# A gate on four column groups, a first norm in blocks of four tiles, and loads behind the identity

## What is computed

```python
x = x + 0.5 * _L0_ffn_ref(_layernorm(x, axis=-1), ...)
x = x + _L0_attn_ref(_layernorm(x, axis=-1), ...)
x = x + 0.5 * _L0_ffn_ref(_layernorm(x, axis=-1), ...)

def _L0_ffn_ref(x, gate_w, gate_b, w1, b1, w2, b2, w3, b3):
    logits = jnp.einsum('bsd,de->bse', x, gate_w) + gate_b
    probs = jax.nn.softmax(logits, axis=1)
    vals, idx = jax.lax.top_k(probs, K)
    ...
```

## Time and profile before

| | us |
|---|---|
| median of 3 runs | 2303.44 (2300.15 to 2309.62) |
| the profiled execution, its own time | 2308.49 |
| its span | 2306.7 |
| PE busy in the span | 2189.5 (95%) |
| DVE busy | 1855.1 (80%) |
| ACT busy | 1608.6 (70%) |
| POOL busy | 534.6 (23%) |

### The profile page before, as it was taken

The page is one execution under the profiler, slowest core; times in us unless marked ns, Lnnn a source line. Parts: engine busy times, 40 slices in busy tenths (PEclk is TensorE's granted clock), DMA queues, the critical chain, the costliest instruction groups (busy, mean ns, idle before and its releaser), DMA issues.

```text
span 2306.7 us, 97898 instructions
## 1 busy us (share of the span) xinstructions
PE 2189.5 (95%) x42417; PEld 1911.3 (83%) x42417; DVE 1855.1 (80%) x3872; ACT 1608.6 (70%) x3516; POOL 534.6 (23%) x1311
## 2 busy tenths in 40 slices
PE   5699988999999999999999999999999998879997
PEld 4588876469899999999999999998999996768885
DVE  4655556599999999999999999999999993465555
ACT  2244444478888888888888888888888886234442
POOL 1233311331221312212212212222122111023330
PEclk7599999999999999999999999999999999769998
DMA  6311112420100100101101001011010003031112
GB/s 201 104 48 46 46 19 72 135 68 8 31 22 13 31 11 25 30 5 32 24 11 31 15 20 31 6 29 27 8 31 22 13 4 112 1 113 48 48 46 81
DMA packets 95464, 96.23 MB, mean 42 GB/s; under 512 B 41269, under 2 KB 84025, under 8 KB 95033
## 3 DMA queue, kind: packets, MB, share of 16 engines
q0 software_dynamic: 42048, 44.80, 7.8%
q1 hardware_dynamic: 52016, 44.10, 6.1%
q10 hardware_dynamic: 968, 1.06, 0.1%
HBM read 64.14 MB, written 25.43 MB: 39 GB/s over the span
## 4 chain that ended last, share of the span: by engine, by line
PE 93%; DVE 3%; ACT 2%; issue 2%; POOL 1%; DMA 0%; ACTq 0%; POOLq 0%; DVEq 0%
PE bank L1016 42%; PE bank L1008 18%; PE bank L917 18%; PE bank L971 2%; PE bank L877 2%; PE bank L1054 2%; PE bank L928 1%; PE bank L984 1%; PE bank L1119 1%; PE bank L855 1%; PE bank L897 1%; PE bank L935 1%; ACT feat L684 1%; PE bank L1062 1%; DVE x_res L1411 0%
## 5 line engine op out<-in xcount | busy, mean ns | idle before, releaser
L1016 PE MATMUL bank<-work 96*32 96x512 bf16 (+4 forms) x17920 | 1415.3, 363 | 4.9 <-DVE work L1450 3.6
L793 ACT ACTIVATE feat<-bank 128x512 f32<-128x512 f32 (+3 forms) x2304 | 1251.4, 565 | 155.3 <-PE bank L1016 78.2
L1450 DVE TENSOR_REDUCE work<-bank 128x1 f32<-128x512 f32 (+3 forms) x2176 | 1299.8, 640 | 64.7 <-PE bank L1016 52.9
L1008 PE MATMUL bank<-feat,phase 128*17 128x128 f32 x16896 | 1138.9, 272 | 1.1 <-issue 1.1
L1008 PEld LDWEIGHTS bank<-feat,phase 128*17 128x17 f32 x16896 | 829.3, 98 | 67.2 <-issue 2.3
L1016 PEld LDWEIGHTS bank<-work 96*32 96x32 bf16 (+1 forms) x17920 | 809.8, 96 | 72.3 <-DVE work L1450 13.2
L917 PE MATMUL bank<-work 128*128 128x256 f32 x1872 | 434.7, 382 | 3.4 <-issue 2.7
L917 PEld LDWEIGHTS bank<-work 128*128 128x128 f32 x1872 | 340.5, 191 | 53.6 <-issue 12.1
L1348 DVE COPY work<-phase 128x514 f32 x234 | 100.6, 430 | 189.6 <-ACT work L742 57.4
L555 POOL TENSOR_SCALAR_AFFINE_SELECT feat<-feat 128x128 f32<-128x128 f32 x512 | 147.2, 295 | 446.0 <-ACT feat L793 437.2
L497 POOL DMA_INDIRECT work<-token_table,row_no x156 | 149.0, 955 | 327.8 <-DVE work L1362 240.9
(11 more groups left out here) (169 smaller groups left out, 1484.2 us busy)
## 6 DMA issues: line engine op xcount, KB each, us to landing
phase<-in_w SPq DMA_DIRECT2D x12, 1024.0 KB, 11.9
work<-qk_parts POOLq DMA_DIRECT2D x60, 192.0 KB, 4.2
token_table<-rows SPq DMA_DIRECT2D x8, 1056.0 KB, 8.8
qk_parts<-phase SPq DMA_DIRECT2D x20, 384.0 KB, 2.6
work<-qk_parts POOLq DMA_DIRECT2D x60, 128.0 KB, 4.5
qk_parts<-work SPq DMA_DIRECT2D x12, 384.0 KB, 3.0
x_res<-in_x SPq DMA_DIRECT2D x4, 1024.0 KB, 13.3
work<-work SPq DMA_DIRECT2D x256, 1.0 KB
```

The source lines that it names most:

```text
L793: eng.activation(p_ring[:, n % P_RING, lo:QB], s_bank("probs", n)[:, lo:QB], ACT.Exp, scale=HD ** -0.5).then_inc(sig.s_done, 1)
L1008: mm = eng.matmul(bank[ACC_BANK][GRID * g:GRID * g + VW, 0:P], v_aug[:, t, h, :], p_ring[:, n % P_RING, g * P:(g + 1) * P], start=(t == 0) ...
L1016: mm = eng.matmul(out[GRID * g:GRID * (g + 1), width], left[:, GRID * g:GRID * (g + 1)], right, start=start, stop=stop)
L1450: eng.tensor_reduce(maxima[:, h % 2, j, i, k + 1:k + 2], scores[:, 0:hi - lo], AX_X, ALU.max).then_inc(sig.a_done, 1)
```

## The change

1. The first norm goes by 8 groups of 4 tiles, and x comes in 8 DMAs of 4 tiles.
2. SP waits after the first of these loads until POOL has built the identity (`ident_at`); seven loads of x, the expert weights, the biases and now `w_qkv_sb` and `w_out_sb`, which were ACT's, come behind that wait. ACT issues the two small gate loads only; the gate's weights wait for a memset of DVE, since they now have 32 columns, of which 24 are zero. The rows of zeros are stored behind the first norm.
3. The transposes wait for the identity alone, no longer for all constants.
4. The gate is turned round. The gate's weights (128x32) stand still, and 128 tokens move; four tiles go to four column groups of PE and four 32-partition strips of bank 2. ACT copies the 128x128 result to `gate_t`, and one matmul per block of four tiles, with `gate_t` as weights against 32 columns of the identity, puts the logits back with tokens on partitions, in bank 7.
5. In both norms with a gate, the gate of a block stands behind other work: in the first norm behind the next block's transposes; in the third behind the output projection of the group after.
6. `H_BANKS` loses bank 7: two banks take turns for the heads' transposes.

```diff
-LN_GRP = (GRP, 4, GRP)
+LN_GRP = (4, 4, GRP)
+GATE_TILES, GATE_W = 4, 32
+GATES = NT // GATE_TILES
-H_BANKS = (3, 6, 7)
+H_BANKS = (3, 6)
...
             triangle(ident[:, :], 0.0, ALU.not_equal, 1.0)
+            ident_at[0] = n_const[0]
...
-            for g in range(GROUPS):
-                eng.dma_start(x_res[:, g * GRP:(g + 1) * GRP, :],
-                              x_rows[:, g * GRP:(g + 1) * GRP, :]).then_inc(sig.x_loaded[g], 16)
+            for g in range(NT // LN_GRP[0]):
+                a, b = g * LN_GRP[0], (g + 1) * LN_GRP[0]
+                if g == 1:
+
+                    need.wait_ge(sig.const, ident_at[0])
+                eng.dma_start(x_res[:, a:b, :], x_rows[:, a:b, :]).then_inc(sig.x_loaded[g], 16)
             load_experts(0)
+            eng.dma_start(w_qkv_sb[:, :, :], w_qkv_t.rearrange("(k p) o -> p k o", p=P)).then_inc(sig.attw, 16)
+            eng.dma_start(w_out_sb[:, :, :], w_out_t.rearrange("(k p) o -> p k o", p=P)).then_inc(sig.attw, 16)
...
         def _(eng):
             need = Waits(eng)
-            eng.dma_start(gate_w_sb[:, :, :], gate_w.rearrange("(k p) e -> p k e", p=P)).then_inc(sig.small, 16)
             eng.dma_start(gate_b_sb[:, :], gate_b.partition_broadcast(P)).then_inc(sig.small, 16)
-            eng.dma_start(w_qkv_sb[:, :, :], w_qkv_t.rearrange("(k p) o -> p k o", p=P)).then_inc(sig.attw, 16)
-            eng.dma_start(w_out_sb[:, :, :], w_out_t.rearrange("(k p) o -> p k o", p=P)).then_inc(sig.attw, 16)
+            need.wait_ge(sig.gate_pad, 1)
+            eng.dma_start(gate_w_sb[:, :, 0:E], gate_w.rearrange("(k p) e -> p k e", p=P)).then_inc(sig.small, 16)
...
+            def copy_gate(f, m):
+
+                need.wait_ge(sig.gate_t[f], m + 1 if f == 0 else m // 2 * 2 + 2)
+                need.wait_ge(sig.gate[f], m - 1)
+                eng.activation(gate_t[:, m % 2, :], bank[2][:, m % 2 * P:(m % 2 + 1) * P],
+                               ACT.Copy).then_inc(sig.gate_copy[f], 1)
+
+            def first_norm():
+                sqrt_of(0, 0)
+                for m in range(GATES):
+                    if m + 1 < GATES:
+                        sqrt_of(0, m + 1)
+                    copy_feat(0, m)
+                    if m:
+                        copy_gate(0, m - 1)
+                copy_gate(0, GATES - 1)
...
             def transpose_rows(n, g):
-                need.wait_ge(sig.const, n_const[0])
+                need.wait_ge(sig.const, ident_at[0])
...
+            def gate(f, m):
+
+                need.wait_ge(sig.small, 32)
+                need.wait_ge(sig.feat[2 * f], KD * (m + 1))
+                need.wait_ge(sig.gate_copy[f], m if f == 0 else m // 2 * 2)
+                if f == 1:
+                    need.wait_ge(sig.s_done, S_ALL)
+                for k in range(KD):
+                    for g in range(GATE_TILES):
+                        i = GATE_TILES * m + g
+                        mm = eng.matmul(bank[2][GATE_W * g:GATE_W * (g + 1), m % 2 * P:(m % 2 + 1) * P],
+                                        gate_w_sb[:, k, :], feat[:, k, i * P:(i + 1) * P], start=(k == 0),
+                                        stop=(k == KD - 1))
+                mm.then_inc(sig.gate_t[f], 1)
+
+            def gate_rows(f, m):
+
+                need.wait_ge(sig.gate_copy[f], m + 1)
+                width = GATE_TILES * E
+                eng.matmul(bank[7][:, m * width:(m + 1) * width], gate_t[:, m % 2, :],
+                           ident[:, :].rearrange("p (c w) -> p c w", c=GATE_TILES)[:, :, 0:E], start=True,
+                           stop=True).then_inc(sig.gate[f], 1)
+
+            def first_norm():
+                for m in range(GATES):
+                    transpose_rows(0, m)
+                    if m:
+                        gate(0, m - 1)
+                    if m > 1:
+                        gate_rows(0, m - 2)
+                gate_rows(0, GATES - 2)
+                gate(0, GATES - 1)
+                gate_rows(0, GATES - 1)
+
             def layer_norm(n, add, consume):
                 add(0)
                 groups = NT // LN_GRP[n]
                 for g in range(groups):
                     if g + 1 < groups:
                         add(g + 1)
+                    if n == 2 and g:
+                        gate(1, 2 * g - 2)
+                        gate(1, 2 * g - 1)
                     transpose_rows(n, g)
+                    if n == 2 and g:
+                        gate_rows(1, 2 * g - 2)
+                        gate_rows(1, 2 * g - 1)
                     consume(g)
+                if n == 2:
+                    gate(1, GATES - 2)
+                    gate(1, GATES - 1)
+                    gate_rows(1, GATES - 2)
+                    gate_rows(1, GATES - 1)
...
-            layer_norm(0, nothing, lambda g: gate(0, g))
+            first_norm()
...
+            def first_norm():
+                statistics(0, 0)
+                for g in range(GATES):
+                    if g + 1 < GATES:
+                        statistics(0, g + 1)
+                    normalise(0, g)
...
-            layer_norm(0, nothing, nothing)
+            eng.memset(gate_w_sb[:, :, :], 0.0).then_inc(sig.gate_pad, 1)
+            first_norm()
```

More of the change, by code:

```diff
@@ L209, in __init__ @@
         self.const = one("constants")
-        self.x_loaded = many("x_loaded", GROUPS)
-        self.small = one("small_loads")
+        self.x_loaded = many("x_loaded", NT // LN_GRP[0])
+        self.gate_pad, self.small = one("gate_padded"), one("small_loads")
         self.attw = one("attention_weights")
@@ L328, in macaron_block @@
         v_rest = sb("v_rest", [P, D])
+        gate_t = v_rest[:, :].rearrange("p (b s) -> p b s", b=2)
         wat = [0]
@@ L658, in _, with store_zero_rows @@
             need = Waits(eng)
-            eng.dma_start(gate_w_sb[:, :, :], gate_w.rearrange("(k p) e -> p k e", p=P)).then_inc(sig.small, 16)
             eng.dma_start(gate_b_sb[:, :], gate_b.partition_broadcast(P)).then_inc(sig.small, 16)
-            eng.dma_start(w_qkv_sb[:, :, :], w_qkv_t.rearrange("(k p) o -> p k o", p=P)).then_inc(sig.attw, 16)
-            eng.dma_start(w_out_sb[:, :, :], w_out_t.rearrange("(k p) o -> p k o", p=P)).then_inc(sig.attw, 16)
-            need.wait_ge(sig.const, zeros_at[0])
-            for f in range(2):
-                eng.dma_start(table[f][0:1, :].rearrange("o (a b) -> (o a) b", a=2),
-                              zeros_bf[:, :].bitcast(F32)[0:2, 0:ROW // 2]).then_inc(sig.zero, 16)
+            need.wait_ge(sig.gate_pad, 1)
+            eng.dma_start(gate_w_sb[:, :, 0:E], gate_w.rearrange("(k p) e -> p k e", p=P)).then_inc(sig.small, 16)
+            def store_zero_rows():
+                need.wait_ge(sig.const, zeros_at[0])
+                for f in range(2):
+                    eng.dma_start(table[f][0:1, :].rearrange("o (a b) -> (o a) b", a=2),
+                                  zeros_bf[:, :].bitcast(F32)[0:2, 0:ROW // 2]).then_inc(sig.zero, 16)
             def sqrt_of(n, g):
@@ L697, in layer_norm @@
                     consume(g)
+                if n == 2:
+                    copy_gate(1, GATES - 2)
+                    copy_gate(1, GATES - 1)
             def nothing(g):
@@ L710, in route @@
                                bc(chosen[:, :, :], 2, [P, NT, V_ROWS // E, E]), ACT.Copy).then_inc(sig.chosen_wide[f], 1)
-                need.wait_ge(sig.gate[f], NT * KD)
+                need.wait_ge(sig.gate[f], GATES)
                 for m in range(NT // 4):
@@ L863, in layer_norm @@
                         add(g + 1)
+                    if n == 2 and g:
+                        gate(1, 2 * g - 2)
+                        gate(1, 2 * g - 1)
                     transpose_rows(n, g)
+                    if n == 2 and g:
+                        gate_rows(1, 2 * g - 2)
+                        gate_rows(1, 2 * g - 1)
                     consume(g)
+                if n == 2:
+                    gate(1, GATES - 2)
+                    gate(1, GATES - 1)
+                    gate_rows(1, GATES - 2)
+                    gate_rows(1, GATES - 1)
             def nothing(g):
                 return
-            def gate(f, g):
-                need.wait_ge(sig.small, 32)
-                need.wait_ge(sig.feat[2 * f], 2 * KD * (g + 1))
-                if f == 1:
-                    need.wait_ge(sig.s_done, S_ALL)
-                for i in range(g * GRP, (g + 1) * GRP):
-                    for k in range(KD):
-                        eng.matmul(bank[2][:, i * E:(i + 1) * E], feat[:, k, i * P:(i + 1) * P], gate_w_sb[:, k, :],
-                                   start=(k == 0), stop=(k == KD - 1)).then_inc(sig.gate[f], 1)
             def route(f):
@@ L882, in route @@
                 need.wait_ge(sig.routed[f], ROUTED["chosen_bf"])
+                need.wait_ge(sig.const, n_const[0])
                 if f == 1:
@@ L1127, in _ @@
             attention()
-            layer_norm(2, attended, lambda g: gate(1, g))
```

(5 more changed lines are left out.)

10 lines of the change are left out of this document (7 added, 3 removed).

## The result

| | before | after |
|---|---|---|
| median of four runs each, us | 2302.44 (2300.15 to 2309.62) | 2265.09 (2264.18 to 2265.92) |
| ratio, 95% interval | | 0.9825 (0.981 to 0.9841) |
| profiled execution, its span | 2308.49, 2306.7 | 2265.92, 2264.2 |
| logits of the first norm (DVE's first routing step) | 64.27 | 45.82 |
| last attention matmul | 1933.98 | 1909.94 |

The change gains 37.4 us by the medians: 18.45 in the first norm and 18.75 in the third. (The profiled pair is 42.6 apart. 5.8 of it lie in attention, 1596.5 us before and 1590.7 after, where the program is the same; they belong to those two executions, see gate_alone_again.)

A forecast was written before the change was run, and what follows sets the result against it. The prediction took PE as the bound in both norms with a gate, and DVE as the first norm's new bound. Gains of 21 us (first norm) and 17 (third), 38 in all, took 2303.4 to 2265.4 us; range 2257 to 2279.

The forecast's parts named there:

- The bound moves to DVE: First norm: with the new gate DVE sets the pace at 3.55 us a block, PE about level at 3.6.
- Rival (b): Gate's column groups do not overlap, or shape changes cost a microsecond: only 10 us gained, 2293 us; chance 0.07.
- (c): Gate's column groups quite serial at low clock, a block costing PE over 6 us: slower, 2317 us; chance 0.02.
- The change of shape: PE at the new gate: switching to column groups and back costs 0.19 us for both changes together.
- The first norm: Logits of the first norm at 43.2 us instead of 64.3: 21 us gained.
- I take half, 6.1: POOL's 12.26 us wait before the identity's select halves to 6.1 without the long loads; identity ready at 7.6 us.
- the "1.0" for POOL's wide copies: First norm: 1.0 us added for DVE's work being slowed beside POOL's wide copies.
- Rival (a): First norm: POOL's wait is its own and stays at 12.26 us; 15 us gained instead of 21, 2271.5; chance 0.27.
- The third norm: Third norm's logits at about 1995.3 us instead of 2012.3: 17 us gained, between 10 and 20.
- The granted clock at 1.00 up to the last projection, and low in the tail: Third norm: PE's clock holds full until the last projection, then is low, costing another 1.5 us.
- its debits: Third norm: 0.6 us once for two head banks, and up to 2 us for ACT's later square root at low clock.
- that walk along PE's list: Third norm: PE's work summed from 1957.05 at full clock, ending the last projection at 1981.0 us instead of 1992.1.

The follow-up runs named there:

- gate_alone_again: Repeat of gate_alone, the same kernel on another chip: 2264.92 us, 0.985 for gate_alone and 0.9835 here, against the kernel before.
- loads_alone: Changed kernel with the old gate's matmuls, in the third norm straight behind their transposes, and three banks for the heads: 2299.27 us, 0.9964 of the kernel before.
- identity_first: Changed kernel with SP's wait for the identity put ahead of the first load of x too: 2261.57 us (one run).
- after_again: The changed kernel, unaltered, run again in another group: 2264.91 us, 0.9835 of the kernel before.
- all_at_once: Changed kernel without SP's wait for the identity, so all loads are issued at once: 2260.38 us, 0.9812 of the kernel before.
- gate_in_place: Changed kernel with the third norm's gate and turning back right behind the transposes they read: 2270.36 us, 0.984 of the kernel before.
- gate_alone: Changed kernel with the kernel before's four loads of x, no SP wait, attention weights in ACT's queue, transposes waiting for all constants: 2273.68 us, 0.985 of before.
- wide_copies_late: Changed kernel with POOL's two wide copies held until DVE has written all rows of the first norm: 2268.42 us, 0.9847 of the kernel before.
- copies_in_gaps: Changed kernel with each of POOL's wide copies waiting for a group of DVE's rows, to meet the next statistics: 2262.56 us, 0.9823 of before.

## Why the prediction was right

The median came out at 2265.09, forecast 2265.4. The sum hides two misses that cancel, and each of its steps had an answer of its own.

**The bound moves to DVE: right.** DVE has no holes from block 1 on, PE waits for it in every block, and loads_alone shows the other side: with the old gate PE stays the bound. Rival (b), column groups that do not overlap, and (c), a block of over 6 us, are out: 16 records take 0.57 us at the higher level and 1.08 at the lower, against 0.55 and 1.1 taken from attention's row. The turning back of two blocks took 0.37 us from start to start in the third norm (1950.12 to 1950.49), 0.19 a block, forecast 0.22.

**The change of shape: right.** The last block's 8 transposes and the change behind them took 1.01 us (41.95 to 42.96) where 8 transposes of the heads take 0.87: 0.14 at most for the change to column groups; the one back lies in the gate's 0.57, taken as 0.55. Both were put at 0.19. The Trainium skill (TensorEngine Tiling (Array Packing), Key Properties) says the array drains at a change; this trace does not contradict it, but shows no price above 0.14 us for the change to column groups.

**The first norm: 18.45 gained, not 21.** The step that failed is the identity: "I take half, 6.1" of the 12.26 us. identity_first shows 6.86 for the part that stays without long loads, and one block of x beside it makes it 8.37 here, and 7.8 to 8.0 in five other kernels with the same loads, after_again among them. That makes the landing of block 1 13.89 instead of 12.0, 2.3 too late by the identity and 0.4 less by the load behind it (3.93 instead of 4.4). The second term that was mis-sized is the "1.0" for POOL's wide copies: it cost 2.4, since it met four rows, not the small operation that the row showed. DVE's blocks of 3.43 instead of 3.55 gave 0.6 back. 2.3 - 0.4 + 1.4 - 0.6 - 0.1 (tail 3.93 instead of 4.0) = 2.6: logits at 45.82, forecast 43.2. Rival (a), the wait unchanged at 12.26, was wrong for these loads, but would have done no harm where DVE had x: all_at_once had 10.98.

**What the prediction did not ask** is whether the wait for the identity is worth its price. It priced parts 2 and 3 as part of one sum, with DVE's start at the landing of block 1, and had both numbers at hand: DVE needs x from the start, the identity only for PE, a block later. gate_alone_again and all_at_once give the answer: the transposes' wait for the identity alone, with the smaller loads, is worth 5.0 us at the logits (44.82 to 39.86), and SP's wait gives 6.0 back (45.82). The 5.0 hold the attention weights' move from ACT's queue to the end of SP's as well: DVE starts block 1 3.1 us earlier, at 8.37 instead of 11.45, and has no wait of 3.5, but loses 1.6 to POOL's copies. The three were not run one by one.

**The third norm: 18.75 gained, not 17.** "The granted clock at 1.00 up to the last projection, and low in the tail" was the wrong way round. It was 0.66 once in the middle, where one projection took 5.41 us instead of 3.7: 1.7 lost, so the last projection ended 48.7 us behind attention's last matmul, 9.4 earlier than before, forecast 11.1. Five of the other kernels did not have that stretch, and gained the 11.1. In the tail it was 1.00: from there to the logits 10.85 us, of which 7.4 DVE's as forecast and 3.43 PE's and ACT's, where the prediction with its debits had 14.3. The gate's place behind a projection, on which that walk along PE's list rests, is worth about 1.9 us of it by gate_in_place, at equal clock. Part of the gain is the clock's: before, the granted clock was 0.73, 0.78, 0.65 and 0.50 in the stretches of 5 us from 1960, 1980, 1995 and 2005, each with an old gate in it; after, it is 1.00 from 1935 to 1970, where all the new gates stand.

**The rest.** What follows moved forward unchanged: from the first logits to the tiles' end it is 273.2 us before (64.27 to 337.49) and 273.4 after (45.82 to 319.25). The weights that SP loads later were not missed.

Open is what sets the stretches of lower granted clock in attention's first 150 us. They come at different places in executions of one kernel: from 420 to 520 us the granted clock was 0.93 in gate_alone, with attention at 1601.1, and 1.00 in the changed kernel, with 1590.7. That they make all of the scatter of up to 10 us between runs is likely, but only profiled runs can show it, and no run here settles what starts them. A third bank for the heads in the changed kernel was not tried, since no bank is free there.

## What to carry to other kernels

Before a wait is added to keep one engine's start free of traffic, ask what the engine that bounds the stretch needs: here DVE needed x and not the identity, and the wait that made the identity 2.6 us earlier cost 6 us. Undo each part of a change that is measured as one; the gate, with DVE's blocks of four tiles, was worth all of it, and what stood beside it was +5 and -6. And where an engine that is off the path does wide work, it matters what it meets on the other engines, and whether a first use behind it was hidden so far.

## What the runs showed of the hardware

- POOL had two stretches without visible cause at the start: 6.86 to 12.26 us before its first affine select, longer with more of x in transfer (6.86, 7.8 to 8.4, 8.7, 10.7 to 11.0), though equal long loads gave 10.5 and 12.3; and 7.73 before its first reduction over the partitions, 5.9 of them with its input ready, seen only where that came right behind other POOL work (wide_copies_late).
- Two bf16 copies on POOL (128x2048 in 1.89 us, 128x1248 in 1.29) stretched four single-precision 128x256 operations of DVE from 1.38 to 3.78 us, and left the statistics of four tiles at 1.40 (copies_in_gaps).
- The old gate took 3.74 to 7.01 us for 8 tiles (32 records with 128 weight columns, 8 moving) by the level of the clock, the new one 1.01 to 1.05 (128 moving, four column groups) at the higher one.
- In loads_alone PE stands in the chain without a hole from 22.1 us to 60.8, and 8 transposes took 1.80 us in it to the last block, where 8 take 0.87 at the higher level; in the changed kernel, with holes, the higher level came at about 29.5 and stayed. The granted clock's column shows 1.00 for loads_alone from 0 to 60 us and for the changed kernel from 15 to 25, where the durations of PE's rows are those of the lower level, so that at a trace's start the level has to be read from the durations.
